# Writing out the loops of attention, routing and experts in a post-norm layer, with nothing loaded behind the last expert

## The chip, the cores and the metric

The kernel runs on one core of a Trainium2 chip. The metric is the device time of one execution, in microseconds (us); lower is better. The five engines of the core are called TensorE (PE, its weight loads PEld), VectorE (DVE), ScalarE (ACT), GpSimd (POOL) and SyncE (SP). Each has its own program and waits for the others by semaphores.

## The reference

A layer of a transformer with the norms behind the blocks, in float32, for 2048 tokens of width 512.

```python
x = layernorm(x + attention(x))   # 16 heads of 128, causal softmax
x = layernorm(x + moe(x))
# attention: k, q, v = W_K x, W_Q x, W_V x per head; masked softmax(q k^T / sqrt(128)) v; then W_O
# moe: 64 experts of inner width 352, softmax gate, top 6 of 64 per token, at most 128 tokens an expert:
#   y_e = (silu(x w1_e^T) * (x w3_e^T)) w2_e^T, weighted by the gate and added to the token's row;
#   and a shared expert of inner width 704 for every token
```

## The kernel before, in words

Three blocks follow each other: `attention`, `route_and_experts` and `combine`. Products keep float32 accuracy by splitting each operand in a rounded part ("hi") and the rest ("lo"): ScalarE makes hi by a copy, VectorE makes lo by a subtraction, and TensorE runs three products for each one wanted (`PASSES`, L42).

**Attention** (L109 to L688) handles the heads in eight pairs. One pair is a fixed list of steps, `ORDER` (L76), which `attention_plan` turns into a plan: projections (L585, L596), scores (L609), exponentials (L392), turns of the probabilities by TensorE (L626) with their hi and lo (L403, L497), products with v (L641), the inverse sums and the store of z. Every engine walks through the same list. The last steps of the list belong already to the next pair ("ahead"); the steps ahead of the first pair are done before the loop. On each engine, `Fori(0, PAIRS - 1)` runs the body for seven pairs, and the last pair's body is written out behind it, without the steps ahead (L338, L434, L542, L686). SP loads a chunk of x into `x_sb` when the last projection that reads the chunk before has been made (L313 to L318).

**Routing** (`step` on each engine) goes through 16 tiles of 128 tokens: output projection (L1385), norm (`normalise`, L1617), turn of x1 (L1397), gate logits, the choice of six experts (`choose`), counts (L1404) and places, and GpSimd's scatter of the rows to the experts' lists in memory (L1008). ScalarE and GpSimd are written out; TensorE, VectorE and SP write out tiles 0 to 3 and 12 to 15 and have a loop of two iterations of four tiles between (L1139, L1560, L1836).

**Experts** run as four bodies of 22 units: 16 experts and six halves of the shared expert, in the order `PATTERN` (L708). A unit's products up go to `h_even` or `h_odd` (L1466); ScalarE makes silu (L1277), VectorE multiplies (L1784), TensorE turns h (L1447), ScalarE and VectorE split it, and TensorE makes the products down (L1506). A body begins with the turn of h of the unit before, the turn of the first expert's rows (L1442), and its products up. An expert's weights come in seven pieces, four of 128x704 and three of up to 128x512 floats, through eight slots of `w_raw` (L1125), each split by ScalarE (L1256) and VectorE (L1756). Which pieces are loaded in a unit says `pieces_of_step` (L723). The last units of a body load seven pieces for the next body's first two experts, six of them 128x704, and the rows of its first expert; in the last body the expert's number is taken modulo 64, so that they are loaded and split again with no use, and SP waits for them at the end (L1186 to L1188). ScalarE scales the result with the gate into one of two buffers `y_sb` (L1320) once the scatter before the last has landed. GpSimd adds it to the tokens' rows in memory by a read-modify-write scatter (L1050), and three times a body the shared expert's rows (L1057); it waits for each to land before the next. TensorE, ScalarE and GpSimd write body 0 out and have a loop for bodies 1 to 3 (L1066, L1363, L1583), as VectorE (L1864); SP's loop has all four (L1172).

In a loop, a wait's value depends on the iteration. The helpers `after` and `done` compute it from the loop's register `i`:

```python
def after(i, per, k):
    return i * per + (per + k)
```

**Combine** (L1881) loads all rows, norms them and stores them. It begins when the block before has ended on all engines, GpSimd's last addition with it.

## Time and profile before

| | us |
|---|---|
| median of three runs | 2666.51 (2664.92 to 2666.80) |
| the profiled execution, its own time | 2663.28 |
| its span, first to last instruction | 2661.6 |
| TensorE busy with matmuls | 2489.5 |
| VectorE busy | 1778.8 |
| ScalarE busy | 1460.7 |
| GpSimd busy | 274.6 |
| mean granted clock of TensorE | 0.975 |

The stages follow each other in time: attention up to 1691 us, routing to about 1996 us (with the first eight units of the shared expert at its end), the expert bodies to 2614 us, the last additions and the combine to 2661.6 us. Times in the rows below are counted from the span's start. "Busy" leaves out register, branch and semaphore instructions and the issue of transfers. In a timeline, the bracket at a line's end is the idle time of that engine just before it and what ended it; "issue" is written where no semaphore of the profile explains the idle time. A granted clock of 1.00 is 2.4 GHz and one of 0.50 is 1.2 GHz; what lies between is a mix of the two.

### The profile page before, as it was taken

Reading aid. Unit: us, or ns where it says so; the run is one execution under the profiler, and the core shown is the slowest. Engines: PE = TensorE matmul, PEld = TensorE weight load, DVE = VectorE, ACT = ScalarE, POOL = GpSimd, SP = SyncE. Lnnn points to the kernel's source line nnn. Section 1 sums busy time; section 2 is a strip of 40 time slices with the busy share of each in tenths; the row PEclk is TensorE's granted clock in tenths of the full one; section 3 lists DMA queues with packets and bytes.
Section 4 is the critical chain, followed back from the end, with each engine's and each line's share of the span. In section 5 each row is a group of like instructions: output and inputs, shape, how many; then the busy total and the mean of one; then the engine's idle time right before and its main releaser. Section 6 shows DMA issues by size and latency. Waiting matters only on the chain. (4 is left out here: it accounts for less than half of the span.)

```text
span 2661.6 us, 47883 instructions
## 1 busy us (share of the span) xinstructions
PE 2489.5 (94%) x14304; PEld 2153.4 (81%) x14304; DVE 1778.8 (67%) x3809; ACT 1460.7 (55%) x3254; POOL 274.6 (10%) x221
## 2 busy tenths in 40 slices
PE   6999999999999999999999999798899999999992
PEld 5888888888888888888888888576688988898992
DVE  3665566566466557557466566588868887787885
ACT  3555555455456456456455455444437776677772
POOL 0000000000000000000000000045541222221120
PEclk8999999999999999999999999899999999999996
DMA  6311311310320321311221120467659999999995
GB/s 245 122 49 48 118 49 51 117 50 21 104 94 15 107 79 32 106 54 54 85 79 54 67 78 17 151 225 262 226 155 285 313 300 278 287 307 294 287 314 187
DMA packets 178147, 383.77 MB, mean 144 GB/s; under 512 B 19689, under 2 KB 52585, under 8 KB 167600
## 3 DMA queue, kind: packets, MB, share of 16 engines
q1 hardware_dynamic: 155248, 333.38, 37.2%
q0 software_dynamic: 20288, 42.59, 7.2%
q10 hardware_dynamic: 2304, 4.20, 0.4%
q8 instruction: 132, 2.16, 0.3%
q14 instruction: 175, 1.43, 0.2%
HBM read 282.37 MB, written 106.35 MB: 146 GB/s over the span
## 5 line engine op out<-in xcount | busy, mean ns | idle before, releaser
L403 ACT ACTIVATE pT_hi<-turned 128x512 fp32r<-128x512 f32 (+3 forms) x640 | 331.1, 537 | 311.0 <-PE turned L626 309.6
L497 DVE TENSOR_TENSOR pT_lo<-turned,pT_hi 128x512 fp32r<-128x512 f32 (+3 forms) x640 | 376.6, 606 | 100.9 <-ACT pT_hi L403 99.6
L392 ACT ACTIVATE probs<-bank,neg_max 128x512 f32<-128x512 f32 (+3 forms) x640 | 396.0, 626 | 80.7 <-DVE neg_max L491 76.9
L483 DVE TENSOR_REDUCE max_part<-bank 128x1 f32<-128x512 f32 (+2 forms) x576 | 347.6, 622 | 108.0 <-PE bank L609 99.2
L596 PE MATMUL bank<-x_sb,w_hi 128*128 128x512 f32 x1024 | 327.3, 401 | 20.5 <-ACT ident_bf L367 13.8
L626 PE MATMUL turned<-ident,probs 128*128 128x128 f32 x2176 | 323.6, 275 | 19.6 <-issue 19.1
L626 PEld LDWEIGHTS turned<-ident,probs 128*128 128x128 f32 x2176 | 265.4, 142 | 64.8 <-issue 20.6
L641 PE MATMUL z_ps<-pT_hi,v_hi 128*128 128x512 f32 (+3 forms) x640 | 255.2, 399 | 15.7 <-DVE pT_lo L497 12.9
L609 PE MATMUL bank<-k_lo,q_hi 128*128 128x512 f32 (+2 forms) x640 | 254.0, 397 | 0.0
L1756 DVE TENSOR_TENSOR up_lo<-w_raw,up_hi 128x704 fp32r<-128x704 f32 x262 | 222.4, 887 | 42.0 <-ACT up_hi L1256 41.3
L609 PE MATMUL bank<-k_hi,q_hi 128*128 128x512 f32 (+2 forms) x640 | 250.4, 391 | 0.0
L596 PEld LDWEIGHTS bank<-x_sb,w_hi 128*128 128x128 f32 x1024 | 194.6, 193 | 60.4 <-issue 13.8
L641 PE MATMUL z_ps<-pT_hi,v_lo 128*128 128x512 f32 (+3 forms) x640 | 233.8, 365 | 0.0
L609 PE MATMUL bank<-k_hi,q_lo 128*128 128x512 f32 (+2 forms) x640 | 233.6, 365 | 0.0
L641 PE MATMUL z_ps<-pT_lo,v_hi 128*128 128x512 f32 (+3 forms) x640 | 233.1, 364 | 0.0
L596 PE MATMUL bank<-x_sb,w_lo 128*128 128x512 f32 x512 | 203.0, 396 | 0.0
L585 PE MATMUL bank<-w_hi,x_sb 128*128 128x256 f32 x1024 | 193.2, 285 | 1.7 <-ACT probs L392 1.7
L1256 ACT ACTIVATE up_hi<-w_raw 128x704 fp32r<-128x704 f32 x256 | 189.0, 785 | 2.2 <-DMA w_raw<-in_w 2.2
L978 POOL MEMSET ident<- 128x128 f32 x1 | 0.2, 204 | 1695.2 <-POOLq L146 1695.2
L585 PEld LDWEIGHTS bank<-w_hi,x_sb 128*128 128x128 f32 x1024 | 163.3, 193 | 3.3 <-DVE probs L456 2.1
L1050 POOL DMA_INDIRECT sums_dram<-y_sb,token x64 | 115.4, 1802 | 396.9 <-DMA sums_dram<-y_sb,token 232.9
L468 DVE TENSOR_TENSOR q_lo<-bank,q_hi 128x512 fp32r<-128x512 f32 x64 | 44.3, 692 | 166.1 <-ACT q_hi L376 164.6
(211 smaller groups left out, 5352.4 us busy)
## 6 DMA issues: line engine op xcount, KB each, us to landing
w_raw<-in_w SPq DMA_DIRECT2D x262, 352.0 KB, 5.6
x_sb<-x_parts SPq DMA_DIRECT2D x62, 1024.0 KB, 6.4
w_raw<-in_w SPq DMA_DIRECT2D x129, 256.0 KB, 5.1
rows_in<-gathered_x SPq DMA_DIRECT2D x65, 263.5 KB, 5.4
gathered_x<-empty_row SPq DMA_DIRECT2D x64, 263.5 KB, 9.2
z_dram<-z_sb SPq DMA_DIRECT2D x64, 256.0 KB, 2.9
z_raw<-z_dram SPq DMA_DIRECT2D x16, 1024.0 KB, 5.6
w_raw<-in_w_qkv SPq DMA_DIRECT2D x32, 384.0 KB, 10.2
```

Source lines behind the costliest of these rows:

```text
L392: nc.scalar.activation(probs[:, u % 2, r, kc * CHUNK:kc * CHUNK + used], bank[:, job_at["s", h, c, r, kc] % BANKS, 0:used], ACT.Exp, bias= ...
L403: nc.scalar.activation(pT_sb[0][:, n % TURNS, lo_col:], turned[:, n % TURNS, lo_col:], ACT.Copy).then_inc(turn_hi, 1)
L483: nc.vector.reduce_max(max_part[:, row % ROWS, kc:kc + 1], bank[:, job % BANKS, 0:used], axis=AX_X).then_inc(part_done, 1)
L497: nc.vector.tensor_tensor(pT_sb[1][:, n % TURNS, lo_col:], turned[:, n % TURNS, lo_col:], pT_sb[0][:, n % TURNS, lo_col:].bitcast(F32), AL ...
L585: mark = nc.tensor.matmul(dst[:, t * 2 * DH:(t + 1) * 2 * DH], x_sb[:, a, dt, rows_], w_sb[b][:, dt, 4 * DH:], start=(dt == 0 and (a, b) = ...
L596: mark = nc.tensor.matmul(dst, w_sb[a][:, dt, first:first + DH], x_sb[:, b, dt, :], start=(dt == 0 and (a, b) == PASSES[0]), stop=(dt == D ...
L609: mark = nc.tensor.matmul(dst[:, 0:width], q_sb[a][:, h, r * P:(r + 1) * P], k_sb[b][:, h, kc * CHUNK:kc * CHUNK + width], start=(a, b) == ...
L626: mark = nc.tensor.transpose(turned[:, n % TURNS, r * P:(r + 1) * P], probs[:, u % 2, r, j * P:(j + 1) * P], ident[:])
L641: mark = nc.tensor.matmul(z_ps[:, first * P:], v_sb[a][:, j, h * DH:(h + 1) * DH], pT_sb[b][:, n % TURNS, first * P:], start=(j == 0 and ( ...
L1050: nc.gpsimd.indirect_dma_start(sums_dram, bass.IndirectOffsetOnAxis(ap=token4[:, n:n + 1], axis=0), y_sb[:, n % 2], None, bounds_check=las ...
L1256: nc.scalar.activation(dst_of(0, n % 2, p, up_w, down_w), raw_of(raw, q % SLOTS_RAW, p), ACT.Copy).then_inc(w_hi, 1)
L1756: nc.vector.tensor_tensor(dst_of(1, n % 2, p, up_w, down_w), raw_of(raw, q % SLOTS_RAW, p), dst_of(0, n % 2, p, up_w, down_w).bitcast(F32) ...
```

## The change

All loops of the three stages become Python loops: each engine's program holds every iteration, and `i` is a number in all of it. So waits are on constants, addresses of transfers are constants, and no jump back is left. `exists` becomes a comparison of numbers. In the last expert body `in_step` leaves out the seven pieces that belong to experts behind the last: SP does not load them, and ScalarE and VectorE do not split them. The rows of a 65th expert are not loaded, and SP's waits for all of these go. The order of the steps within an iteration is unchanged on each engine.

```diff
@@ -58,7 +58,7 @@
 def exists(i, k):
-    return not isinstance(i, int) or 0 <= k < TILES
+    return 0 <= i * NB + k < TILES
@@ -335,9 +335,8 @@
-            with sp.Fori(0, PAIRS - 1) as i:
-                body(i, False)
-            body(PAIRS - 1, True)
+            for i in range(PAIRS):
+                body(i, i == PAIRS - 1)
...
@@ -572,7 +569,7 @@
                     pe.wait_ge(x_in, i * (32 * CHUNKS) + 32 * c)
-                elif isinstance(i, int):
+                elif i < 0:
                     pe.wait_ge(x_lo, DT)
...
@@ -683,9 +680,8 @@
-            with pe.Fori(0, PAIRS - 1) as i:
-                body(i, False)
-            body(PAIRS - 1, True)
+            for i in range(PAIRS):
+                body(i, i == PAIRS - 1)
@@ -748,6 +743,10 @@
+    def in_step(i, u):
+
+        return [pieces.index(piece) for piece in pieces_of_step[u] if i * NE + piece[0] < EXPERTS]
@@ -1040,10 +1039,10 @@
-                if n or not isinstance(i, int):
+                if n or i:
                     pool.wait_ge(y_stored[(n - 1) % 2], i * (16 * NE // 2) + 16 * ((n - 1) // 2 + 1))
...
@@ -1063,8 +1062,7 @@
-            body(0)
-            with pool.Fori(1, BODIES) as i:
+            for i in range(BODIES):
                 body(i)
@@ -1130,18 +1128,13 @@
-                e = (i * NE + n) % EXPERTS if n == NE else i * NE + n
+                e = i * NE + n
...
-            for k in range(NB):
-                step(0, k)
-            with sp.Fori(0, LOOPS) as i:
-                for k in range(NB, 2 * NB):
-                    step(i, k)
-            for k in range(TILES - NB, TILES):
+            for k in range(TILES):
                 step(0, k)
@@ -1169,23 +1162,17 @@
-            with sp.Fori(0, BODIES) as i:
+            for i in range(BODIES):
                 for u, (kind, n) in enumerate(UNITS):
-                    if u + 1 == NU or UNITS[u + 1][0] == "e":
+                    if u + 1 == NU and i + 1 < BODIES or u + 1 < NU and UNITS[u + 1][0] == "e":
                         load_rows(i, NE if u + 1 == NU else UNITS[u + 1][1])
...
-                    for piece in pieces_of_step[u]:
-                        q = pieces.index(piece)
-
+                    for q in in_step(i, u):
                         sp.wait_ge(w_lo, after(i, NQ, q - SLOTS_RAW + 1))
-
-                        load_piece((i * NE + piece[0]) % EXPERTS if piece[0] >= NE else i * NE + piece[0], q)
-            for slot_ in range(SLOTS_RAW):
-                sp.wait_ge(raw_in[slot_], PER_SLOT * (BODIES + 1))
-            sp.wait_ge(rows_loaded[0], 16 * (EXPERTS // 2 + 1))
+                        load_piece(i * NE + pieces[q][0], q)
@@ -1329,7 +1316,7 @@
-                    loads = [pieces.index(piece) for piece in pieces_of_step[u]]
+                    loads = in_step(i, u)
...
@@ -1580,9 +1561,8 @@
-            body(0, True)
-            with pe.Fori(1, BODIES) as i:
-                body(i, False)
+            for i in range(BODIES):
+                body(i, i == 0)
```

The loops of ScalarE and VectorE in attention, of TensorE and VectorE in routing, and of ScalarE and VectorE in the experts change in the same manner.

## Rows read from the trace of the kernel before

**Rows 1.** The page, part 1: busy us (share of the span) xinstructions of each engine

```profile
PE 2489.5 (94%) x14304; PEld 2153.4 (81%) x14304; DVE 1778.8 (67%) x3809; ACT 1460.7 (55%) x3254; POOL 274.6 (10%) x221
```

**Rows 2.** Waits of TensorE: engine, line, releaser: us in total, times, longest us

```profile
PE turned L626 <- issue: 19.1, 6, 3.5
```

**Rows 3.** Timeline of TensorE, attention: start us, us, instruction [idle before <-releaser]

```profile
258.37 1.20 PE L626 MATMUL turned<-ident,probs 128*128 128x128 f32 x9 [3.07 <-issue]
...
392.13 0.47 PE L641 MATMUL z_ps<-pT_hi,v_hi 128*128 128x512 f32 x1 [0.65 <-DVE pT_lo L497]
...
465.22 2.18 PE L626 MATMUL turned<-ident,probs 128*128 128x128 f32 x9 [3.01 <-issue]
...
1300.83 1.63 PE L626 MATMUL turned<-ident,probs 128*128 128x128 f32 x9 [3.53 <-issue]
...
1506.13 1.17 PE L626 MATMUL turned<-ident,probs 128*128 128x128 f32 x9
...
1639.72 0.47 PE L641 MATMUL z_ps<-pT_hi,v_hi 128*128 128x512 f32 x1 [0.61 <-DVE pT_lo L497]
```

**Rows 4.** Windows, TensorE alone, behind a gap: length, busy, granted clock, DMA share, GB/s

```profile
1301.00:1305.00 4.00, 4.00 (x16) 0.57 0.04 10
```

**Rows 5.** Windows, last pair: length, busy PE, PEld, DVE, ACT, POOL, clock, DMA share, GB/s

```profile
1506.00:1507.00 1.00, 1.00 (x12) 1.00 (x11) 0.63 (x1) 1.00 (x4) 0.00 (x0) 1.00 0.00 0
```

**Rows 6.** Timeline of TensorE, expert bodies 0 to 3: their first turns

```profile
2002.94 0.60 PE L1442 MATMUL t_even<-ident,rows_in 128*128 128x128 f32 x4
...
2144.85 0.49 PE L1447 MATMUL t_even<-ident,h_sb 128*128 128x128 f32 x3
...
2151.30 0.60 PE L1442 MATMUL t_even<-ident,rows_in 128*128 128x128 f32 x4
...
2301.02 0.54 PE L1447 MATMUL t_even<-ident,h_sb 128*128 128x128 f32 x3 [0.31 <-issue]
...
2313.03 0.60 PE L1442 MATMUL t_even<-ident,rows_in 128*128 128x128 f32 x4
...
2455.32 0.54 PE L1447 MATMUL t_even<-ident,h_sb 128*128 128x128 f32 x3 [0.27 <-issue]
...
2467.45 0.60 PE L1442 MATMUL t_even<-ident,rows_in 128*128 128x128 f32 x4
...
2609.54 0.49 PE L1447 MATMUL t_even<-ident,h_sb 128*128 128x128 f32 x3
```

**Rows 7.** Timelines of GpSimd, ScalarE and TensorE in expert body 1

```profile
2177.90 1.55 POOL L1050 DMA_INDIRECT sums_dram<-y_sb,token  x1 [6.45 <-DMA sums_dram<-y_sb,token]
...
2186.40 2.08 POOL L1050 DMA_INDIRECT sums_dram<-y_sb,token  x1 [6.95 <-DMA sums_dram<-y_sb,token]
...
2227.99 0.69 ACT L1320 ACTIVATE y_sb<-y_ps,gate 128x512 f32<-128x512 f32 x1 [6.61 <-DMA sums_dram<-y_sb,token]
...
2232.16 0.90 PE L1447 MATMUL t_even<-ident,h_sb 128*128 128x128 f32 x3 [5.00 <-DVE h_sb L1784]
```

**Rows 8.** Windows, all engines, in expert bodies 0 and 2 (columns as in Rows 5)

```profile
2003.00:2144.00 141.00, 139.92 (x823) 129.25 (x822) 119.54 (x235) 104.81 (x202) 26.79 (x17) 1.00 1.01 308
...
2301.00:2455.00 154.00, 148.29 (x856) 136.77 (x856) 125.01 (x247) 109.20 (x210) 32.38 (x20) 0.98 0.98 297
```

**Rows 9.** Timelines of GpSimd and ScalarE at the experts' end

```profile
2599.06 2.54 POOL L1050 DMA_INDIRECT sums_dram<-y_sb,token  x1 [5.93 <-ACT y_sb L1320]
...
2604.28 0.68 ACT L1320 ACTIVATE y_sb<-y_ps,gate 128x512 f32<-128x512 f32 x1
...
2608.63 1.56 POOL L1050 DMA_INDIRECT sums_dram<-y_sb,token  x1 [7.03 <-issue]
...
2610.51 0.68 ACT L1320 ACTIVATE y_sb<-y_ps,gate 128x512 f32<-128x512 f32 x1
...
2614.31 1.55 POOL L1050 DMA_INDIRECT sums_dram<-y_sb,token  x1 [4.12 <-DMA sums_dram<-y_sb,token]
```

**Rows 10.** Timeline of VectorE where the routing loop jumps back

```profile
1825.31 0.69 DVE L1627 TENSOR_TENSOR x<-o_ps,xr 128x512 f32<-128x512 f32 x1 [0.95 <-DVE slot L1697]
```

More of the change, by code:

```diff
@@ L541, in _ @@
                     maximum(-1, *step[2:])
-            with dve.Fori(0, PAIRS - 1) as i:
-                body(i, False)
-            body(PAIRS - 1, True)
+            for i in range(PAIRS):
+                body(i, i == PAIRS - 1)
         @block.tensor
@@ L555, in take @@
             def take(i, n, last):
-                start = isinstance(i, int) and i < 0
+                start = i < 0
                 m = n - BANKS
@@ L660, in left_out @@
                 m = n
-                while m > first_ahead and (last and jobs[m - 1][1] or isinstance(i, int) and i < 0 and not jobs[m - 1][1]):
+                while m > first_ahead and (last and jobs[m - 1][1] or i < 0 and not jobs[m - 1][1]):
                     m -= 1
@@ L685, in _ @@
                 pe.sem_inc(job_ready, left_out(-1, n_jobs, False))
-            with pe.Fori(0, PAIRS - 1) as i:
-                body(i, False)
-            body(PAIRS - 1, True)
+            for i in range(PAIRS):
+                body(i, i == PAIRS - 1)
 def route_and_experts(nc, z_dram, w_o, gate_w, x_rows, w13, w2, s13, s2, sums_dram, x1T_parts, gathered_x):
     BIG = 1 << 20
-    LOOPS = TILES // NB - 2
     GROUP = 2
@@ L1041, in add_rows @@
             def add_rows(i, n):
-                if n or not isinstance(i, int):
+                if n or i:
                     pool.wait_ge(y_stored[(n - 1) % 2], i * (16 * NE // 2) + 16 * ((n - 1) // 2 + 1))
                 s = tile_after.get((n - 1) % NE)
-                if s is not None and (n or not isinstance(i, int)):
+                if s is not None and (n or i):
                     stored = slot_count(i, s, 16) if n else i * 32 + 16 * (FIRST // 2 + s // 2 - 1)
@@ L1316, in result @@
                     per = 16 * NE // 2
-                    if not isinstance(i, int) or i or n >= 2:
+                    if i or n >= 2:
                         act.wait_ge(y_stored[n % 2], i * per + (16 * (n // 2) - (per if wrapped else 0)))
@@ L1362, in _ @@
                 lead_turned(v - 1)
-            body(0, True)
-            with act.Fori(1, BODIES) as i:
-                body(i, False)
+            for i in range(BODIES):
+                body(i, i == 0)
             turned(BODIES, ("h", NU - 1))
@@ L1381, in project @@
                 for h in heads:
-                    if isinstance(i, int) and k == 0 and h % GROUP == 0:
+                    if k == 0 and h % GROUP == 0:
                         pe.wait_ge(wo_split, h // GROUP + 1)
@@ L1557, in _ @@
             pe.wait_ge(gw_in, 16)
-            for k in range(NB):
-                step(0, k)
-            with pe.Fori(0, LOOPS) as i:
-                for k in range(NB, 2 * NB):
-                    step(i, k)
-            for k in range(TILES - NB, TILES):
+            for k in range(TILES):
                 step(0, k)
@@ L1582, in _ @@
             lead_down(LEAD - 2)
-            body(0, True)
-            with pe.Fori(1, BODIES) as i:
-                body(i, False)
+            for i in range(BODIES):
+                body(i, i == 0)
             turn(BODIES, ("h", NU - 1))
@@ L1801, in body @@
                     shared_result(i, (u - 2) % NU, u < 2, first)
-                    loads = [pieces.index(piece) for piece in pieces_of_step[u]]
+                    loads = in_step(i, u)
                     for q in loads[:3]:
@@ L1833, in _ @@
             dve.wait_ge(dve_const, 4)
-            for k in range(NB):
-                step(0, k)
-            with dve.Fori(0, LOOPS) as i:
-                for k in range(NB, 2 * NB):
-                    step(i, k)
-            for k in range(TILES - NB, TILES):
+            for k in range(TILES):
                 step(0, k)
@@ L1863, in _ @@
                     lead_result(v // 2 - 1)
-            body(0, True)
-            with dve.Fori(1, BODIES) as i:
-                body(i, False)
+            for i in range(BODIES):
+                body(i, i == 0)
             turned(BODIES, ("h", NU - 1))
```

1 line of the change is left out of this document (removed).

## The prediction

> **What bounds the kernel now.** I read the page's busy line first: TensorE's matmuls are busy for 94% of the span, and no other engine passes 67% [rows 1]. A change can pay only where TensorE stands still, or by moving the end. So the next view is TensorE's waits. Its largest entry is 19.1 us in 6 pieces that end in "issue", before the turns of L626 [rows 2]. Six is the number of times the attention loop jumps back (seven iterations, L686), so I looked for the places in TensorE's timeline. Each gap stands exactly before the first step of an iteration, and the step that follows the loop, the written-out last pair, starts at 1506.13 us with no gap [rows 3]. The jump back is what costs, not the loop's end. The third view is the same for the experts: bodies 2 and 3, which begin with a jump back, have longer heads than body 1, into which the program falls [rows 6]. Last come the granted clock just behind a gap [rows 4], the queue of the scatters [rows 7, 9] and the DMA share [rows 8].
>
> **The change, part by part.**
>
> Attention. TensorE's gaps are 3.0 to 3.5 us each, 19.1 together [rows 2, 3]. They cost more than that: behind the gap that ends at 1300.83 the granted clock is 0.57, which is mostly the 1.2 GHz level, while the engine had been busy before it stopped [rows 4]. I price both together. From where iteration 1 would have begun without its gap (258.37 - 3.07 = 255.30) to the written-out pair at 1506.13 pass 1250.8 us in six iterations. Iteration 1 kept its clock, and less the gap behind it lasted 465.22 - 3.01 - 258.37 = 203.8 us. Six of these are 1223.0, so **27.8 us** go, 19.1 idle and 8.7 clock. The constants by themselves bring nothing that I can find: from an iteration's first step to the same wait on pT_lo the loop needs 392.13 - 258.37 = 133.8 us, the written-out pair 1639.72 - 1506.13 = 133.6 [rows 3]. TensorE's queue hides the arithmetic of the waits; if that cover were thin it would be worth 6 x 0.2 = 1 us more.
> What was hidden by the gap: the load of x for the next pair. Before the last pair, where there is no gap, DMA traffic has already ended at 1506 us, while the first product that reads x stands behind the nine turns that start at 1506.13 and take 1.17 [rows 3, 5]. About 1 us of slack is left, so nothing new waits here, and I bound the risk by 6 x 1 = 6 us.
>
> Routing. VectorE's chain of small dependent operations sets this stage, and the loop jumps back once. There VectorE idles 0.95 us before L1627 [rows 10], so the jump is worth at most that; this loop's body of four tiles shows no gap of 3 us. Eight of the 16 tiles wait on registers. Attention's 134 us of such waits came out 0.2 us longer than with constants [rows 3], but there TensorE hid them and here nothing does, so I allow up to 0.25 us a tile. I take **1.5 us** for both, bounds 0 and 3.
>
> Experts. The head of a body runs from its first turn of h to the turn of rows for the next unit. In body 1 it takes 2151.30 - 2144.85 = 6.45 us, in bodies 2 and 3 12.01 and 12.13, and a further 0.31 and 0.27 of "issue" stand before these [rows 6]. The remainder of a body shows no gain from constants: body 0, already written out, takes 2144.85 - 2002.94 = 141.9, body 2 takes 2455.32 - 0.27 - 2313.03 = 142.0, body 3 2609.54 - 2467.45 = 142.1. So two jumps are worth 5.6 + 5.7 + 0.6 = **11.8 us**. The written-out body falls to 6.45 + 142 = 148.4 us. Register arithmetic for DMA addresses on SP and POOL goes too; both queues wait for other engines, so I count it at nothing, and it stays nothing if that cover goes, since issues take 0.3 us of the 9 an expert has.
>
> What is late next. The stage's DMA share is 1.01 at 308 GB/s in body 0, and body 2, gap included, needs 154 us at 297 GB/s, 45.7 MB; in 148.4 us that is 308 GB/s, just what body 0 carried [rows 8]. So the data can come, but nothing is over, and the first to feel it is POOL's chain of read-modify-write scatters, one in flight at a time. Under load they follow each other by 8.5 us (2177.90 to 2186.40); in body 1 the chain fell behind, ScalarE waited 6.61 us for a scatter before it could write y_sb, and TensorE stood 5.00 us [rows 7]. With the slower clock behind it, body 1's remainder lasts 2301.02 - 0.31 - 2151.30 = 149.4 against 142.0: **7.4 us** a stall. Bodies 2 and 3 had none, but their jumps had given the chain 6 us to catch up. Body 1 is the one body that begins as all will begin, and body 0 runs at the same pace without a stall. I take one new stall in two bodies: **7.4 us back**, bounds 0 and 14.8; body 1's own stall could go as well, 7.4 in favour.
> The Trainium skill (Perfetto Trace Analysis, Engine Utilization) gives 358 GB/s as a core's HBM peak. By it the stage has a seventh to spare and no stall would be added, which is the first rival below; no row here shows such a rate over a body.
>
> End. Seven weight pieces (six of 352 KB, one of 256 KB) and a block of rows are loaded behind the last expert and seven pieces split on both ScalarE and VectorE. The splits lie beside TensorE's last units and are free. The loads are not: the end is POOL's chain. The scatter issued at 2599.06 under those loads holds back the next until 2608.63, 9.57 us, while the following takes 5.68, with the loads gone [rows 9]. The second's y_sb is written by 2604.28 + 0.68 = 2604.96, so it can go at about 2605.1. The third is bound by its own y_sb at 2611.2 instead of 2614.31: **3.0 us** off the end, bounds 0 and 3.5.
>
> Sum: 27.8 + 1.5 + 11.8 + 3.0 = 44.1, less 7.4 = 36.7 us. The profiled execution took 2663.3 us, so it would take 2626.6; the median of the three runs, 2666.5, is 3.2 above it, which I add: about **2629.5 us**.
>
> **Rivals.**
> *No new stall* in the experts, or body 1's goes too: 44 to 51.5 us, 2615 to 2622. For it: body 0's 308 GB/s without a stall. Against: body 1.
> *Two new stalls* and, in attention, a late x: 29.3 down to 23.3 us, 2637 to 2643. For it: full DMA queues; against it: the remainders of bodies 0, 2 and 3 last 142 us alike, so none of them holds a stall at this pace [rows 6].
> *The gaps stay.* "Issue" says only that no semaphore explains the gap. If it were the engine's reading of its own instructions, which a written-out program reads too, only routing's and the end's few us would go: 2662 to 2664. The Trainium skill speaks for this (Advanced Engine Details and Errata, Control Flow Timing): it prices a taken branch at about 0.05 us and a compare-and-branch at 0.11. By that the nine jumps are worth 1 us in all and 3 us gaps need another cause. Against it: entries without a jump, at 1506.13 and 2144.85, have no gap although they too go on to instructions never read before.
> *Slower.* The place is POOL's chain in bodies 1 to 3: 19 transfers a body, each behind the one before. They took 464.7 us, from 2144.85 to 2609.54 [rows 6]. If the traffic, pressed together, stretches the mean spacing to 9.0 us, between the 8.5 seen and the 9.57 at the end, the chain is the bound: 57 x 9.0 = 513, 48 us more, against 32.3 won elsewhere: 2682. It ends slower only from a mean over (464.7 + 32.3 + 5.3) / 57 = 8.8 us. At a mean of 8.5 it would still be 12.5 us faster.
>
> **How the numbers follow.** Forecast (one new stall) 0.42; none 0.30; two or more 0.20; gaps stay 0.05; slower 0.03. A measurement of this kernel tells about 0.2%, 5.3 us. Faster by more: 0.42 + 0.30 + 0.20 and a little of the rest, 0.93; within, 0.05; slower, 0.02. The range takes forecast and both neighbours with their bounds: 2613 to 2645.
>
> **What would show it.** TensorE's waits hold no "issue" of 3 us before L626, and the pairs' first turns stand 203.5 to 204 us apart. The heads of expert bodies 2 and 3 are 6.4 to 6.5 us. If a stall is added, ScalarE's y_sb waits some 6 us for a scatter at a second place besides that of [rows 7]. The last scatters follow by at most 6.2 us. I am wrong if gaps of 3 us remain at fixed steps, if DMA waits appear before L596, or if an expert body without a scatter stall takes over 150 us.

## The result and the profile after

After the change the kernel takes 2613.1 us, the median of four runs (2611.5 to 2617.5), against 2665.7 us before (four runs, 2658.3 to 2666.8). The ratio is 0.9816, 95% interval 0.9803 to 0.9829: 52.6 us less, or 1.8%. The forecast was 2629.5 us with a range of 2613 to 2645, so the time lies at the low edge of the range, and the first rival of the prediction, without a new stall in the experts, comes nearer.

The profiled execution after the change took 2612.1 us. The page begins:

```profile
span 2610.3 us, 40937 instructions
...
PE 2474.8 (95%) x14304; PEld 2141.0 (82%) x14304; DVE 1762.7 (68%) x3802; ACT 1454.5 (56%) x3247; POOL 268.6 (10%) x221
...
q8 instruction: 115, 1.88, 0.3%
q14 instruction: 89, 0.73, 0.1%
...
L623 PE MATMUL turned<-ident,probs 128*128 128x128 f32 x2176 | 320.5, 273 | 0.3 <-PEq L682 0.3
```

The turns of attention, now L623, had 19.1 us of "issue" before them [rows 2] and have none: their whole idle time is 0.3 us. TensorE's busy time fell too, 2489.5 [rows 1] to 2474.8 us with the same 14304 matmuls. The work is the same, and the mean granted clock rose from 0.975 to 0.983. The two queues that carry instructions moved 115 packets of q8 and 89 of q14. The same two lines of the page of before are (packets, MB, share):

```profile
q8 instruction: 132, 2.16, 0.3%
q14 instruction: 175, 1.43, 0.2%
```

A written-out program thus reads fewer instruction bytes than the looped one did, 2.61 MB against 3.59. About half of the difference is that it runs fewer instructions. 2.61 MB for 40937 are 64 bytes each, so every instruction is read once; the page of before counts 47883, since the waits of a loop need register instructions, and at 64 bytes these would be 3.06 MB. The other 0.53 MB were read although no instruction more was run. That is the first hint at what the gaps were.

To see where the 51.3 us of span went, I put one mark into each stage: the same instruction in both timelines of TensorE. After the change:

```profile
182.96 0.47 PE L638 MATMUL z_ps<-pT_hi,v_hi 128*128 128x512 f32 x1 [0.61 <-DVE pT_lo L495]
386.41 0.47 PE L638 MATMUL z_ps<-pT_hi,v_hi 128*128 128x512 f32 x1 [0.61 <-DVE pT_lo L495]
...
1607.51 0.47 PE L638 MATMUL z_ps<-pT_hi,v_hi 128*128 128x512 f32 x1 [0.61 <-DVE pT_lo L495]
...
1679.09 0.76 PE L1371 MATMUL o_ps<-wo_hi,z_hi 128*128 128x512 f32 x1 [14.69 <-DVE wo_lo L1589]
...
1966.74 0.40 PE L1452 MATMUL h_even<-up_hi,eT_hi 128*128 128x352 f32 x1 [1.49 <-issue]
...
2028.65 0.40 PE L1452 MATMUL h_odd<-up_hi,eT_hi 128*128 128x352 f32 x1 [1.27 <-DVE up_lo L1736]
...
2118.17 0.40 PE L1452 MATMUL h_even<-up_hi,eT_hi 128*128 128x352 f32 x1 [1.50 <-issue]
...
2264.00 0.49 PE L1433 MATMUL t_even<-ident,h_sb 128*128 128x128 f32 x3
...
2266.42 0.40 PE L1452 MATMUL h_even<-up_hi,eT_hi 128*128 128x352 f32 x1 [1.50 <-issue]
...
2270.32 0.60 PE L1428 MATMUL t_even<-ident,rows_in 128*128 128x128 f32 x4
...
2414.94 0.40 PE L1452 MATMUL h_even<-up_hi,eT_hi 128*128 128x352 f32 x1 [1.49 <-issue]
...
2562.50 0.50 PE L1492 MATMUL ys_ps<-s_down_hi,hT_hi 128*128 128x512 f32 x1 [1.29 <-DVE hT_lo L1743]
```

And before it:

```profile
185.21 0.47 PE L641 MATMUL z_ps<-pT_hi,v_hi 128*128 128x512 f32 x1 [0.65 <-DVE pT_lo L497]
...
1708.32 0.76 PE L1385 MATMUL o_ps<-wo_hi,z_hi 128*128 128x512 f32 x1 [14.88 <-DVE wo_lo L1609]
...
1999.02 0.40 PE L1466 MATMUL h_even<-up_hi,eT_hi 128*128 128x352 f32 x1 [1.46 <-issue]
...
2147.38 0.42 PE L1466 MATMUL h_even<-up_hi,eT_hi 128*128 128x352 f32 x1 [1.61 <-DVE eT_lo L1774]
...
2306.84 0.65 PE L1466 MATMUL h_even<-up_hi,eT_hi 128*128 128x352 f32 x1 [4.84 <-DVE eT_lo L1774]
...
2461.98 0.66 PE L1466 MATMUL h_even<-up_hi,eT_hi 128*128 128x352 f32 x1 [5.68 <-DVE eT_lo L1774]
...
2611.32 0.50 PE L1506 MATMUL ys_ps<-s_down_hi,hT_hi 128*128 128x512 f32 x1 [1.28 <-DVE hT_lo L1763]
```

From these marks, with the 1639.72 of [rows 3]:

| stretch | before | after | gain | forecast |
|---|---|---|---|---|
| start to the first pair's mark | 185.21 | 182.96 | 2.3 | none |
| seven pairs | 1454.51 | 1424.55 | 30.0 | 27.8 |
| last pair's end, first product of wo | 68.60 | 71.58 | -3.0 | 0 |
| routing, to the first expert's product | 290.70 | 287.65 | 3.1 | 1.5 |
| four expert bodies | 612.30 | 595.76 | 16.5 | 11.8 - 7.4 |
| the end | 50.28 | 47.80 | 2.5 | 3.0 |
| sum | 2661.6 | 2610.3 | 51.3 | 36.7 |

Attention is regular now: a pair takes 203.5 us (386.41 - 182.96), seven take 7 x 203.5. The head of expert body 2, from its turn of h at 2264.00 to the turn of rows at 2270.32, is 6.3 us, where it was 12.0 [rows 6]. The four bodies last 151.4, 148.3, 148.5 and 147.6 us; before, 148.4, 159.5, 155.1 and 149.3. ScalarE's y_sb has no wait for a scatter at all, so the stall of [rows 7] is gone, and no new one has come.

Two things went the wrong way, and both are small. Body 0 is 3.1 us longer than before: a split of weights came late at 2028.65. And behind the last pair TensorE's clock fell where it had been full before. The windows (length, busy PE, PEld, DVE, ACT, POOL, clock, DMA share, GB/s) at the same point of the program, 32 us behind the mark, after:

```profile
1640.00:1642.00 2.00, 2.00 (x11) 1.90 (x9) 0.55 (x3) 0.49 (x2) 0.00 (x0) 0.52 0.00 0
```

and before:

```profile
1672.00:1674.00 2.00, 2.00 (x17) 1.97 (x18) 0.81 (x5) 0.88 (x2) 0.00 (x0) 1.00 0.03 8
```

Clock 0.52 is nearly all the 1.2 GHz level, and the engine gets 11 matmuls done in the time of 17. In front of it, in 1638 to 1640 us, it was busy 1.26 of 2 us at full clock, and before the change 1.04 of 2 in the like place. Nothing in that shows why one fell and the other didn't, and the other executions below, looped or not, have this stretch at anything from 68.2 to 71.6 us. So I take it for chance and for no part of the change; that is not shown.

### The profile page after: what moved, and what is told of

The parts are those of the page before. It is cut to its first block and busy times, and to the rows that moved or that the text cites. A ratio compares the mean times of both kernels' runs of the same rounds, so it can differ in the third digit from the quotient of the medians.

```text
span 2610.3 us, 40937 instructions
## 1 busy us (share of the span) xinstructions
PE 2474.8 (95%) x14304; PEld 2141.0 (82%) x14304; DVE 1762.7 (68%) x3802; ACT 1454.5 (56%) x3247; POOL 268.6 (10%) x221
## 5 line engine op out<-in xcount | busy, mean ns | idle before, releaser
L593 PE MATMUL bank<-x_sb,w_hi 128*128 128x512 f32 x1024 | 323.4, 397 | 20.1 <-ACT ident_bf L366 13.6
L623 PE MATMUL turned<-ident,probs 128*128 128x128 f32 x2176 | 320.5, 273 | 0.3 <-PEq L682 0.3
L623 PEld LDWEIGHTS turned<-ident,probs 128*128 128x128 f32 x2176 | 263.1, 141 | 44.9 <-issue 0.7
L593 PEld LDWEIGHTS bank<-x_sb,w_hi 128*128 128x128 f32 x1024 | 191.7, 190 | 59.1 <-issue 13.6
L593 PE MATMUL bank<-x_sb,w_lo 128*128 128x512 f32 x512 | 201.4, 393 | 0.0
L638 PEld LDWEIGHTS z_ps<-pT_hi,v_hi 128*128 128x128 f32 x640 | 121.2, 189 | 36.6 <-DVE pT_lo L495 14.1
L1049 POOL DMA_INDIRECT sums_dram<-y_sb,token x64 | 110.0, 1720 | 386.5 <-DMA sums_dram<-y_sb,token 244.1
```

Source lines behind the costliest of these rows:

```text
L593: mark = nc.tensor.matmul(dst, w_sb[a][:, dt, first:first + DH], x_sb[:, b, dt, :], start=(dt == 0 and (a, b) == PASSES[0]), stop=(dt == D ...
L623: mark = nc.tensor.transpose(turned[:, n % TURNS, r * P:(r + 1) * P], probs[:, u % 2, r, j * P:(j + 1) * P], ident[:])
L638: mark = nc.tensor.matmul(z_ps[:, first * P:], v_sb[a][:, j, h * DH:(h + 1) * DH], pT_sb[b][:, n % TURNS, first * P:], start=(j == 0 and ( ...
L1049: nc.gpsimd.indirect_dma_start(sums_dram, bass.IndirectOffsetOnAxis(ap=token4[:, n:n + 1], axis=0), y_sb[:, n % 2], None, bounds_check=las ...
```

## Experiments

The theory after the first reading: the gaps were jumps back of TensorE to code that is not at hand, so that its own instructions had to be fetched; in the expert bodies the jumps of ScalarE and VectorE did the same. Rivals: the jumps of the other engines made TensorE wait; the arithmetic on registers for the waits; the jump as an instruction, wherever it leads; and, in the experts, that POOL's chain of scatters sets the time of a stall.

**Attention's loops back, all four and one by one.** The edit, at the end of `attention` for each engine named, everything else as after the change:

```diff
-            for i in range(PAIRS):
-                body(i, i == PAIRS - 1)
+            with pe.Fori(0, PAIRS - 1) as i:
+                body(i, False)
+            body(PAIRS - 1, True)
```

All four engines (for ScalarE, VectorE and SyncE the same with act, dve, sp):

> The changed kernel with attention alone put back into loops, on all four engines that have one. My theory: six far jumps on TensorE cost 3.2 us of idle and 1.5 us of slower clock each, and the waits on registers 0.35 us a pair, so about 30 us come back: 2643 us, with six gaps of 3.0 to 3.5 us before L626's turns. Rival, that most of the gain came from the experts and the end: 2620 us or less.

TensorE alone:

> Only TensorE's attention loop comes back; SyncE, ScalarE and VectorE stay written out. My theory is that TensorE's own jump sets the cost and hides the others': the same 2641 to 2643 us as with all four loops. Rival, that the engines' gaps add up or that a gap of ScalarE or VectorE sets the pace: 2625 us or less.

SyncE, ScalarE and VectorE, TensorE written out:

> TensorE stays written out; SyncE, ScalarE and VectorE loop in attention. My theory: their gaps of about 3 us fall beside TensorE's nine turns and a projection of 5.5 us, so that at most 1 us a pair is seen: 2613 to 2620 us. Rival, that theirs count as well: 6 x 3 us or more, 2631 us or more.

No loop, but on all four engines the pair's number in a register, so that every wait and address is worked out as in the loop:

```diff
-            for i in range(PAIRS):
-                body(i, i == PAIRS - 1)
+            for p in range(PAIRS - 1):
+                body(nc.snap(nc.tensor.to_reg(p), min_val=0, max_val=PAIRS - 2), False)
+            body(PAIRS - 1, True)
```

> Attention is written out for each pair, with no jump, but the pair's number sits in a register, so that each wait and address is computed as in the loop (840 register instructions on TensorE in place of none). My theory: 0.35 us a pair, 2.4 us in all: 2615 to 2616 us, and no gap of 3 us. Rival, that the register arithmetic makes the gaps: 2640 us.

Measured, the first four on one chip with seven runs of the kernel before (median 2662.4), the last line being the kernel after the change from its own measurement:

| attention | median, us | ratio, 95% interval | seven pairs by the marks | gaps on TensorE |
|---|---|---|---|---|
| all in loops | 2641.6 | 0.9892 to 0.9940 | 1453.8 | 6 |
| TensorE in a loop | 2638.2 | 0.9878 to 0.9943 | 1451.0 | 6 |
| the others in loops | 2612.6 | 0.9785 to 0.9837 | 1425.4 | none |
| written out, registers | 2611.6 | 0.9774 to 0.9824 | 1425.9 | none |
| written out, constants | 2613.1 | 0.9803 to 0.9829 | 1424.6 | none |

The kernel after the change was not run again with the experiments, here or below, and the median of the kernel before moved between 2662.3 and 2665.7 us from one group to the next. So a difference of a few us against 2613.1 is read from the timelines and not from the medians.

The waits of TensorE (us in total, times, longest) and the page's instruction queue when TensorE alone loops:

```profile
PE turned L623 <- issue: 17.0, 6, 3.1
...
q8 instruction: 130, 2.13, 0.3%
```

and the instruction queues when only the others loop:

```profile
q8 instruction: 115, 1.88, 0.3%
q14 instruction: 139, 1.14, 0.1%
```

The gaps come with TensorE's loop and go with it. The loops of the other three cost 0.8 us over seven pairs, although their jumps are just as many. The queues say what a gap is. With TensorE's loop q8 carries 15 packets of 16 KB more than written out; with the loops of the others q14 carries 50 packets of 8 KB more, and q8 none. Part of both is the register instructions. The run with registers and no jump has, with 44637 instructions:

```profile
q8 instruction: 118, 1.93, 0.3%
q14 instruction: 113, 0.93, 0.1%
```

So 3 of the 15 packets and 24 of the 50 belong to the registers. What is left on q8 is 12, two for each of TensorE's six jumps. The trace also has the time of each packet. The instruction queue in the gap of TensorE that ends at 1294.97, in the kernel where TensorE alone loops (window 1292.22 to 1294.97 us):

```profile
q8 instruction: 1, 0.02, 2.2%
```

It is the same at every gap. In the four kernels whose TensorE jumps back without a hint (before, all in loops, TensorE alone, and the three loops below) there are 21 gaps, and in each exactly one packet of q8 begins, 0.1 to 0.9 us behind the gap's start; the first turn follows 2.5 to 3.0 us behind the packet's start. The two longest gaps, 3.53 and 3.35 us, are those whose packets begin latest, 0.9 and 0.8 us in. So the engine reads a block of its code again at each jump back, and stands until it is there. The others read some of theirs again too, but they have slack. Registers cost 1.4 us over seven pairs by the marks, 0.2 us each; the medians, 2611.6 and 2613.1, do not show so little.

**Is it the jump, or where it leads?** A short loop of one wait that has long been met, ahead of each of TensorE's eight pairs: seven taken jumps back within code that is at hand.

```diff
             def body(i, last):
+                with pe.Fori(0, 8):
+                    pe.wait_ge(pool_const, 3)
                 for step in steps_of(last):
```

> The changed kernel, and in front of each of TensorE's eight pairs a loop of eight turns round one wait that is already met: seven jumps back over a few instructions per pair, 56 in all, beside the sequencer's entry and exit. If a taken jump as such costs 3 us, 56 of them cost some 170 us: 2780 us. My theory, that only a jump to instructions that are no longer at hand costs it: some tenths of a us each at most, in part hidden by the work queued ahead: 2613 to 2625 us.

It took 2630.8 us (ratio 0.9868 to 0.9908). That is more than I thought, but far from what 56 jumps of 3 us would add, 168 us. In the timeline the pairs are headed by short gaps:

```profile
1079.30 1.18 PE L623 MATMUL turned<-ident,probs 128*128 128x128 f32 x9 [2.11 <-issue]
```

2.1 us for seven jumps is 0.3 us each, the loop's entry and exit and the draining of TensorE's queue included, against 2.7 to 3.5 for one far jump. The first of the eight gaps, at the start of the kernel, is 3.3 us long, the others 2.1 to 2.3, and in seven of the eight no packet of q8 begins. Between the marks the pairs last 205.7 to 205.8 and 207.3 to 207.7 us in turn, that is 2.2 us more or 3.8 to 4.2. The granted clock tells them apart: in the 4 us behind the gap it is 0.61 to 0.64 in the three longer pairs and 1.00 in the others, so that the gap costs 1.6 to 1.9 us again in clock. A stop of 2 us thus lost the clock at times, as the 3 us gaps did [rows 4].

The Trainium skill (Advanced Engine Details and Errata, Control Flow Timing) has 0.11 us for a compare-and-branch. The short jumps are a factor of three above that, with the wait, the count and the queue in it; the far jumps are a factor of 25 to 32 above. For the far jump the Trainium skill's page Runtime: NRT & Kernel Launch (Instruction fetch mechanics) fits: it says that the instruction buffer is filled ahead in sequence only, in blocks of 16 KB, and that a taken branch out of the two blocks at hand has to fetch its target before the engine can go on. The packets of TensorE's queue agree: 2.13 MB in 130 packets are 16 KB each, and each far jump is followed by the read of one. Those of q14 are smaller, 0.73 MB in 89, 8 KB each. The page gives no time for the stall.

**The far jumps with a hint, and half as many.** The loops of all four engines with a hint on the back edge: one instruction more in each iteration (44697 in all against 44669, that is seven on each of four engines), which announces the jump back:

```diff
-            for i in range(PAIRS):
-                body(i, i == PAIRS - 1)
+            with nc.Fori(0, PAIRS - 1, engines=..., hint_back_edge=True) as i:
+                body(i, False)
+            body(PAIRS - 1, True)
```

Three loops of two pairs one behind the other, and the last two pairs written out, so that there are three jumps back in place of six:

```diff
-            for i in range(PAIRS):
+            for p in range(0, PAIRS - 2, 2):
+                with pe.Fori(p, p + 2) as i:
+                    body(i, False)
+            for i in range(PAIRS - 2, PAIRS):
                 body(i, i == PAIRS - 1)
```

> Attention as three loops of two pairs each and two pairs written out: three jumps back instead of six, six of eight pairs on registers. My theory: 3 x 4.6 + 6 x 0.35 = 16 us above the changed kernel: 2629 us. If the cost went with the waits on registers or with entering a loop, it would be near a1's 2643 us.

Three jumps: 2631.4 us (0.9871 to 0.9913), seven pairs in 1436.9 us, 12.3 more than written out or 4.1 a jump, the registers' share with it, and just three gaps:

```profile
PE turned L632 <- issue: 9.2, 3, 3.3
```

```profile
1505.52 0.47 PE L609 MATMUL bank<-k_hi,q_hi 128*128 128x512 f32 x1 [2.08 <-ACT probs L392]
...
1546.88 0.47 PE L641 MATMUL z_ps<-pT_hi,v_hi 128*128 128x128 f32 x1 [4.29 <-DVE pT_lo L497]
...
1546.53 0.29 DVE L497 TENSOR_TENSOR pT_lo<-turned,pT_hi 128x128 fp32r<-128x128 f32 x1 [5.02 <-issue]
```

VectorE stood 5.0 us on "issue", and TensorE waited 4.3 of them for its pT_lo. The other wait, of 2.1 us, is for ScalarE, which had stood 3.5 us until 1504.7. Both lie in the last pair, 29 and 71 us behind its first step at 1475.73, and in each stop one packet of q14 begins (1503.07 and 1544.67 us). An explanation would be that the hint is wrong the one time the loop ends, and that the two engines then have to read what follows late. q14 carries the code of four engines, so that the packets do not prove it, and it was not tried by itself.

**Which engine's jump made the long heads of the expert bodies?** Bodies 1 and 2 in a loop, with one jump back; body 3 written out. For ScalarE and VectorE:

```diff
-            for i in range(BODIES):
-                body(i, i == 0)
+            body(0, True)
+            with dve.Fori(1, BODIES - 1) as i:
+                body(i, False)
+            body(BODIES - 1, False)
```

> The kernel after the change, but ScalarE and VectorE run expert bodies 1 and 2 in a loop again (one jump back, into body 2); body 3 and everything else stay written out. My theory: the long heads of the expert bodies in the kernel before (12.0 and 12.1 us against 6.4) were the jumps of ScalarE and VectorE, not TensorE's. Then the head of body 2 is about 12 us, TensorE's waits there end in VectorE (4 to 6 us), heads of bodies 1 and 3 stay at 6.4, and the time is 2613.1 + 5.7 = about 2618 to 2620 us. Rival: TensorE's own jump made them long; then the head stays 6.4 us and the time is 2612 to 2615.

For TensorE alone, in the same form:

> The kernel after the change, but TensorE alone runs expert bodies 1 and 2 in a loop (one jump back). My theory: in the kernel before TensorE stood 0.3 us at such a jump, since it was behind VectorE there anyway and its own gap lay beside the others'. Alone, it would stand between 0.3 us (nothing to fetch) and 3 us (as in attention, if its jump costs the same everywhere and was hidden by VectorE's). With 3 us the fetch theory of attention holds for this body as well: gap of 2.7 to 3.3 us ending in issue at the start of body 2, time 2616 to 2618. With 0.3 us: 2613 to 2614.

By the medians both say little: 2616.2 us (0.9792 to 0.9837) and 2615.3 (0.9799 to 0.9844), 3.1 and 2.2 us above the kernel after the change, within what the intervals allow. Both profiles also hold stalls of the kind treated below, one of 2.4 us in the first and two of 1.3 to 1.4 in the second. The timelines at the start of body 2 decide. With the loops of ScalarE and VectorE:

```profile
2261.86 0.49 PE L1435 MATMUL t_even<-ident,h_sb 128*128 128x128 f32 x3
...
2265.41 0.38 ACT L1281 ACTIVATE hT_hi<-t_even 128x256 fp32r<-128x256 f32 x1 [3.62 <-issue]
...
2267.31 0.63 PE L1454 MATMUL h_even<-up_hi,eT_hi 128*128 128x352 f32 x1 [4.52 <-issue]
...
2273.79 0.60 PE L1430 MATMUL t_even<-ident,rows_in 128*128 128x128 f32 x4
```

and with TensorE's:

```profile
2264.27 0.54 PE L1433 MATMUL t_even<-ident,h_sb 128*128 128x128 f32 x3 [2.34 <-issue]
...
2272.29 0.60 PE L1428 MATMUL t_even<-ident,rows_in 128*128 128x128 f32 x4
```

ScalarE stands 3.6 us on "issue", TensorE 4.5 behind it, and the head is 2273.79 - 2261.86 = 11.9 us, just the 12.0 of before. Label and cause differ here: TensorE's wait is put down as "issue" too, though its own code is written out here and only the other two can have held it. VectorE's first step there waits 3.06 us for ScalarE's hT_hi, so it is ScalarE's stop that opens this chain, and two packets of q14 begin in it; what VectorE's jump would cost alone was not tried. TensorE's own jump costs less but not nothing: a gap of 2.3 us, less than the 2.7 to 3.3 expected, and a head of 8.0 us in place of 6.3, at a granted clock of 0.50 between 2267 and 2270 us, 4.0 us together. The gap is shorter than in attention because work was left in TensorE's queue: the block's read begins at 2261.30, before the gap, and the first turn follows 3.0 us behind it. In the kernel before the reads began at 2298.19 and 2452.56, 2.8 us ahead of the first turns [rows 6], and the queue covered all but 0.3. My reading of before, that 0.3 us was all that TensorE's jump cost in the experts, was thus wrong as a price of the jump. There it lay beside the jumps of the others; the three overlap, and the sum, 5.6 to 5.9 us, is about the largest of them. The jumps of SyncE and GpSimd in this block were not tried.

**What the scatters have left.** Two small memsets on POOL ahead of each of the 64 scatters, waited for:

```diff
                 wait_apart(pool, waited4, y_read, after(i, NE, n + 1))
+                for m in range(2):
+                    nc.gpsimd.memset(z_pad[:], 0.0).then_inc(delay, 1)
+                    pool.wait_ge(delay, 2 * (i * NE + n) + m + 1)
                 nc.gpsimd.indirect_dma_start(
```

> The kernel after the change with two small memsets on POOL, each waited for, ahead of each of the 64 scatters, which makes the chain of scatters longer by some 0.5 to 1 us an expert. It measures what the chain has left. My theory: in body 1 the chain runs at 7.8 us a transfer, 19 in 148.4 us, that is with nothing over, and so the bodies become longer: 16 x 0.7 = 11 us a body in the three full bodies, less what little waiting for ScalarE is left; time 2630 to 2650, with ScalarE waiting for scatters in each body. Rival: the chain has slack that spacing under load hides, since a scatter slows down only when many weights are in flight; then the time rises by the occasional stall only, 2613 to 2621.

The 12 adds of the shared expert's tiles, which stand in the same chain, replaced by a small store, so that this kernel leaves them out of the sum:

```diff
-                pool.dma_start(sums_dram[...], ys_sb[:, tile_slot(s)],
-                               accum_op=ALU.add).then_inc(ys_stored[tile_slot(s)], 16)
+                pool.dma_start(unused[:, 0:P], ys_sb[:, tile_slot(s), 0:P]).then_inc(ys_stored[tile_slot(s)], 16)
```

> The kernel after the change with the scatter chain relieved: the 12 adds of the shared expert's tiles that stand between the scatters (256 KB read-modify-write, 7 to 9 us each) are replaced by a plain store of 64 KB to a buffer that nobody reads, so the shared expert's part is left out of 12 tiles of the sum. My theory: the stall that some executions show, about 82 to 84 us into a body, where ScalarE waits for a scatter behind the second of these adds, is POOL's chain falling behind; relieved, it is gone in the trace, the runs lie closer together, and the median falls by 0 to 3 us against 2613.1, to 2610 to 2613. Rival: the stalls come from the weights' traffic; then they stay as often as now, and the time is 2613 to 2616.

The longer chain took 2625.6 us (0.9839 to 0.9884), the shorter 2608.0 (0.9768 to 0.9810). In the first a scatter is issued 1.08 us later by the memsets, 17 us a body, and the bodies last 153.0, 154.5, 156.0 and 147.6 us. The timelines of POOL and TensorE in body 1:

```profile
2183.14 0.91 POOL L1060 DMA_DIRECT2D sums_dram<-ys_sb  x1 [6.82 <-DMA sums_dram<-y_sb,token]
2190.28 0.78 POOL L1051 MEMSET z_pad<- 128x320 f32 x2 [6.24 <-issue]
2191.34 1.82 POOL L1053 DMA_INDIRECT sums_dram<-y_sb,token  x1 [0.28 <-POOL z_pad L1051]
...
2201.42 0.52 PE L1437 MATMUL t_even<-ident,h_sb 128*128 128x128 f32 x3 [4.29 <-DVE h_sb L1768]
```

Bodies 0, 1 and 2 now hold a stall each, of 2.3, 4.3 and 4.8 us on TensorE, each some 18 to 20 us behind the second of the shared expert's adds, which is issued 63 to 67 us into the body (here 2183.14) and after the change at 59 to 60. So POOL's chain is what makes them. But 17 us more of chain lengthened these bodies by 5 to 8 us only, body 3 not at all, and the kernel by 12.5, between what the two theories gave. A body thus had 9 to 12 us to spare, the last one 17. Part of it is POOL's waiting for y_sb, 64.9 us in ten waits over all bodies after the change. In body 1 there is no such wait, and yet the mean spacing of its 19 transfers rose from 7.8 to 8.2 us only, with 1.08 us of memsets ahead of 16 of them. So there the scatters themselves landed sooner when they went out later; why stays open.

The same stall is in other profiles, by chance. Nine of them, the kernel after the change and the runs above and below that left the experts written out and the chain as it is, have 27 bodies 1 to 3. Eight hold one of 1.2 us or more on TensorE and four a smaller one of 1.0 to 1.1, always 81 to 84 us behind the body's first product; none of the nine bodies 0 does. The run with hints has one in each of its three bodies. The run with registers in attention has one in body 1:

```profile
2195.69 0.69 ACT L1311 ACTIVATE y_sb<-y_ps,gate 128x512 f32<-128x512 f32 x1 [5.51 <-issue]
...
2199.96 0.87 PE L1437 MATMUL t_even<-ident,h_sb 128*128 128x128 f32 x3 [3.99 <-DVE h_sb L1768]
```

ScalarE waits 5.5 us to write y_sb, which a scatter still reads, and the chain ends in TensorE's 4.0 us. Its body 1 lasts 154.7 us against 148.3, so a full stall costs 6.4. Over the nine profiles the eight cost some 37 us and the four smaller some 7, on average 4.9 an execution. That is likely part of why the runs of one kernel spread by up to 12 us, and why the shorter chain, which had no such stall in its profile, lies 5.1 us below the kernel after the change, more than I expected. Three other profiles have no stall either, so that one profile does not show that the shorter chain keeps them away; its runs spread by 5.4 us, against 6.0 after the change. Part of the 5.1 may be its smaller traffic, or the difference between the groups of runs; these were not taken apart.

**The useless loads kept.** Everything written out, but the seven pieces, the rows and the splits behind the last expert are still loaded and made, from experts that exist:

```diff
-        return [pieces.index(piece) for piece in pieces_of_step[u] if i * NE + piece[0] < EXPERTS]
+        return [pieces.index(piece) for piece in pieces_of_step[u]]
...
-                        load_piece(i * NE + pieces[q][0], q)
+                        load_piece((i * NE + pieces[q][0]) % EXPERTS, q)
```

> All loops written out, but the seven useless weight pieces, their splits and the useless block of rows are kept at the end. My theory: they delay the last scatters only: 3 us, 2616 us, and the scatter issued under the loads takes over 8 us to the next one. Rival, that they cost TensorE or the splitting engines nothing and the end nothing: 2613 us.

It took 2615.6 us (0.9809 to 0.9844), 2.5 more than without them, which the medians alone do not resolve. POOL's last transfers with the loads kept:

```profile
2561.06 1.99 POOL L1049 DMA_INDIRECT sums_dram<-y_sb,token  x1 [5.97 <-issue]
2567.11 1.55 POOL L1049 DMA_INDIRECT sums_dram<-y_sb,token  x1 [4.07 <-DMA sums_dram<-y_sb,token]
2572.52 0.91 POOL L1056 DMA_DIRECT2D sums_dram<-ys_sb  x1 [3.86 <-DMA sums_dram<-y_sb,token]
```

and after the change:

```profile
2557.38 1.56 POOL L1049 DMA_INDIRECT sums_dram<-y_sb,token  x1 [4.66 <-issue]
2563.14 1.55 POOL L1049 DMA_INDIRECT sums_dram<-y_sb,token  x1 [4.20 <-ACT y_sb L1307]
2568.60 0.92 POOL L1056 DMA_DIRECT2D sums_dram<-ys_sb  x1 [3.90 <-DMA sums_dram<-y_sb,token]
```

With the loads the last scatter waits for the one before it; without, for its own y_sb. Measured from the shared expert's product just before (2563.21 and 2562.50), the last add is issued after 9.3 and 6.1 us: the mechanism of the prediction, and its size. The scatter that I expected to take over 8 us to the next one, issued at 2553.54, took 7.5; the one before it took 9.0.

## Why the prediction was right, and where it was off

The place, the direction and most of the size held; the total, 36.7 us forecast against 51.3 in the profiled execution, was short, and one step accounts for most of that. That the median lies in the range at all is luck: it is 2613.1, and the range ended at 2613.

- **Attention's gaps** were forecast as 27.8 us from TensorE's jump back. The marks give 30.0, and the loops put back cost 28.5 us by the medians (2641.6 - 2613.1). The idle part was right, 19.1 us: no "issue" is left before the turns. The term was 2 us short, and the registers are likely most of it: I had compared the stretch to one wait, 133.8 against 133.6, found 0.2 us and called it hidden. The run with registers and no jump gives 0.2 us a pair, 1.4 in all, where I had allowed at most 1.
- **The late x** did not come. The pairs are 203.5 us each, and no wait for x stands before L593 but the first.
- **The gaps stay**, the rival with the branch's price, fell: in the written-out kernel none is left. Its thought that reading instructions is what takes the time was right all the same. What it missed is that this code, read in sequence, came without a stop, and that a jump back began a read that nothing had begun before: in the 21 gaps the packet starts inside the gap, and with the hint 8 us ahead.
- **Routing** was put at 1.5 us within 0 to 3; the marks give 3.1 with what follows it up to the first expert. In the other twelve profiles routing is written out as well, and there the same stretch lasts 287.0 to 290.3 us against 290.7 before, so that the gain is not clear of chance. No run took this stage by itself, and it stays open what the jump and the registers cost there.
- **The heads of the experts** were 11.8 us, and that held: the head of body 2 fell from 12.0 to 6.3. The cause lay in ScalarE and VectorE, whose jumps, without TensorE's, bring 11.9 back. TensorE's jump, which I read as 0.3 us, costs 4.0 when it stands alone.
- **The added stall** is the step that failed: "I take one new stall in two bodies: 7.4 us back", while body 1's own was kept. In the profiled execution there was no stall, so 14.8 us lie between the two. Body 0 gave 3.1 of them back, so the experts gained 16.5 us where 4.4 were forecast, 12.1 more; the other terms make up the rest of 51.3 - 36.7 = 14.6. The mechanism is real, as the longer chain shows, and the place was right, but I took the one stall in one profile as a property of a body that starts without a pause. It comes in some executions and not in others, 12 in 27 bodies with the small ones, and costs 4.9 us an execution on average, where my forecast had 14.8. The pace that I expected was reached: bodies 1 and 2 carry 308 GB/s at a DMA share of 1.00 and 1.01, without a stall.
- **The slower rival**, a mean spacing of 8.8 us in POOL's chain, fell too. With 19 transfers in 148.3 us the spacing is 7.8 in body 1, where POOL never waits for y_sb. The 8.5 us that I took for the pace under load were one pair of scatters.
- **The end** was 3.0 us; the marks give 2.5 and the loads kept cost 2.5. The last scatters were to follow by at most 6.2 us, and one took 7.2 (2550.20 to 2557.38).
- **Not foreseen**: 2.3 us at the start, 3.0 lost to the clock behind the last pair, 3.1 lost in body 0 to late weights. The first two vary in all the profiles (the first pair's mark lies between 181.0 and 185.2 us) and nearly cancel. The third meets a sign that I had named of being wrong, an expert body without a scatter stall of over 150 us: body 0 took 151.4. The wait at fault, 1.3 us for a split of weights 62 us into the body, comes at the same place in body 0 of the run with the loops of ScalarE and VectorE and in body 1 of the run with all of attention in loops, and at another place in the run with the shorter chain; what makes the weights late was not looked for.

## What to carry to other kernels

When an engine that sets the time shows a regular idle time in "issue" at each turn of a loop, and none where the loop is entered or left, suspect that it is reading its own code again. The packets of the instruction queues settle it: look whether one begins in each gap. The label alone does not, since TensorE's wait in the expert bodies was put down as "issue" when only the others looped. Write the loop out on the engine that waits, or hint its back edge, and look at each loop by itself: in attention TensorE alone was worth 25 of the 28 us and the others had slack, while the long heads of the expert bodies came from the loops of the others. And before a stall in one profile goes into a sum, look whether it is in a second execution: one that comes and goes belongs into the forecast with its mean and into the range at its full size.

## What the runs showed of the hardware that I had not expected

- A far jump back costs TensorE 2.7 to 3.5 us of idle time, and with the clock and the registers 4.1 to 4.4 us (12.3 us for three, 26.4 for six); a jump to code at hand cost 0.3 us on average. In the idle time one 16 KB packet of code is read, and work starts 2.5 to 3.0 us behind its start.
- The hint on the back edge takes the whole gap away, at six jumps of six: the block is read 8 us ahead. In the last pair, behind the loop, VectorE then stood 5.0 us and ScalarE 3.5.
- VectorE and ScalarE stand at far jumps as well, 3.6 to 4.7 us in the expert bodies (the two rows below are VectorE's in the kernel before, at its two jumps), but in attention it is hidden: 0.8 us for 18 such jumps.
- Stops of 2.1 to 2.3 us cost TensorE's clock at every second pair (0.61 to 0.64 behind them against 1.00), though the pairs were alike.
- A written-out program reads less code, 2.61 MB, than the looped one, 3.59 MB: every instruction that is run is read once, in a loop too, the looped one runs 47883 in place of 40937, and each jump back of TensorE reads two packets of 16 KB more.

```profile
2305.50 0.42 DVE L1761 TENSOR_TENSOR hT_lo<-t_even,hT_hi 128x256 fp32r<-128x256 f32 x1 [3.85 <-issue]
...
2460.63 0.42 DVE L1761 TENSOR_TENSOR hT_lo<-t_even,hT_hi 128x256 fp32r<-128x256 f32 x1 [4.67 <-issue]
```
